# A four-stage transformer block on one Trainium2 core: wavelet and gate chains that overlap, keys chosen before the first FFN ends, fewer scores ahead, one mask product for two edges

## The reference

```python
x = x + wavelet(ln(x))     # q and v products, Haar transform over tokens, product of bands, back, W_out
x = x + ffn(ln(x))         # softmax over 8 experts, the top 2 kept; relu(x W1)^2 W2 of each
x = x + attention(ln(x))   # 16 heads of 8: a band of 128, the 128 top keys, the first 64 keys
x = x + ffn(ln(x))         # as the second stage
```

## Time and profile before

| | |
|---|---|
| Median of 3 runs | 576.11 us (575.75 to 577.48) |
| The profiled execution | 576.57 us, span 574.7 us |
| PE busy | 519.8 us, 90% |
| VectorE busy | 407.0 us, 71% |
| ACT busy | 350.0 us, 61% |
| GpSimd busy | 271.6 us, 47% |
| DMA | 32.01 MB, mean 56 GB/s |

### The profile page before, as it was taken

One profiled execution on the slowest core, in us unless ns is written; L12 is line 12 of the kernel. 1 busy time (PEld: TensorE's weight loads), 2 busy tenths in 40 slices (PEclk: granted clock), 3 DMA queues, 4 the chain that ended last, 5 costly groups with the idle time before them and its releaser, 6 DMA issues.

```text
span 574.7 us, 13509 instructions
## 1 busy us (share of the span) xinstructions
PE 519.8 (90%) x4611; PEld 326.3 (57%) x4611; DVE 407.0 (71%) x1458; ACT 350.0 (61%) x775; POOL 271.6 (47%) x429
## 2 busy tenths in 40 slices
PE   5899999999895799889998999999998999889996
PEld 2477777766663464445444554455545554477875
DVE  2545666668999789999977869878688785144335
ACT  6477665756541147656865576776765657666763
POOL 1401101430702996754426987659926346264540
PEclk9999999999897779999999999999999999999999
DMA  7970000000000000000000000001100011575606
GB/s 231 348 249 2 1 1 1 0 2 2 11 2 0 14 14 11 7 15 13 14 4 14 13 14 4 15 14 33 34 3 15 12 45 43 190 255 168 211 19 184
DMA packets 33444, 32.01 MB, mean 56 GB/s; under 512 B 7250, under 2 KB 28502, under 8 KB 33376
## 3 DMA queue, kind: packets, MB, share of 16 engines
q1 hardware_dynamic: 31616, 27.80, 15.7%
q0 software_dynamic: 1760, 3.35, 1.6%
HBM read 8.57 MB, written 12.00 MB: 36 GB/s over the span
## 4 chain that ended last, share of the span: by engine, by line
PE 57%; DVE 27%; issue 7%; POOL 3%; ACT 3%; DMA 1%; SPq 0%; DVEq 0%; POOLq 0%; ACTq 0%
PE BANK L1526 7%; PE BANK L1544 7%; DVE QST L1210 5%; PE BANK L1594 4%; PE BANK L1643 4%; PE BANK L1618 3%; PE BANK L1615 3%; DVE SW L1164 3%; PE BANK L1646 3%; PE BANK L1480 2%; PE BANK L1490 2%; DVE M L1162 2%; PE BANK L1649 2%; DVE QST L1213 2%; DVE X L1146 2%
## 5 line engine op out<-in xcount | busy, mean ns | idle before, releaser
L808 ACT ACTIVATE PT<-BANK 128x256 f32<-128x256 f32 (+2 forms) x352 | 158.6, 491 | 98.7 <-PE BANK L1618 76.0
L540 POOL TENSOR_SCALAR OH<-IOTA,POS 128x128 bf16<-128x128 bf16 x240 | 140.3, 608 | 1.6 <-DVE POS L1178 1.0
L1205 DVE CUSTOM_DVE_ANT_0 XN_a<-BANK,BANDQ 128x256 f32<-128x256 f32 (+1 forms) x128 | 62.5, 488 | 23.1 <-PE BANK L1594 20.4
L1544 PEld LDWEIGHTS BANK<-W,PT 128*128 128x128 f32 x512 | 62.5, 193 | 15.7 <-issue 14.9
L1205 DVE CUSTOM_DVE_ANT_0 XN_c<-BANK,BANDQ 128x384 f32<-128x384 f32 (+1 forms) x128 | 62.3, 487 | 8.9 <-PE BANK L1594 7.7
L1615 PE MATMUL BANK<-BANDK,IDB 128*128 128x128 bf16 x384 | 64.0, 222 | 0.6 <-ACT PT L808 0.3
L1544 PE MATMUL BANK<-W,PT 128*128 128x128 f32 x512 | 62.8, 276 | 0.0
L1526 PE MATMUL BANK<-XNT_ALL,W 128*128 128x512 f32 x128 | 62.0, 609 | 0.0
L719 ACT ACTIVATE PT<-BANK 128x512 f32<-128x512 f32 x64 | 38.0, 598 | 32.3 <-PE BANK L1526 31.7
L1615 PEld LDWEIGHTS BANK<-BANDK,IDB 128*128 128x128 bf16 x384 | 33.7, 98 | 40.2 <-ACT PT L808 22.1
L547 POOL TENSOR_TENSOR SUM<-NRM 128x128 f32<-128x128 f32 x16 | 7.3, 458 | 104.0 <-DVE NRM L1226 104.0
(11 more groups left out here) (298 smaller groups left out, 1170.7 us busy)
## 6 DMA issues: line engine op xcount, KB each, us to landing
xs<-W SPq DMA_DIRECT2D x1, 6984.0 KB, 25.5
KZB<-W SPq DMA_DIRECT2D x16, 256.0 KB, 2.4
KZC<-W SPq DMA_DIRECT2D x15, 256.0 KB, 2.3
QKV<-xs SPq DMA_DIRECT2D x31, 72.0 KB, 1.9
W<-w SPq DMA_DIRECT2D x2, 1024.0 KB, 8.6
X<-x SPq DMA_DIRECT2D x4, 256.0 KB, 3.2
out<-X SPq DMA_DIRECT2D x4, 256.0 KB, 2.2
KZB<-KALL SPq DMA_DIRECT2D x20, 36.0 KB, 1.9
```

What stands on the lines that cost most here:

```text
L540: last = nc.gpsimd.tensor_scalar(OH[g % 2][:, i, t, :], IOTA[:, :], POS[:, t, c:c + 1], None, ALU.is_equal)
L808: nc.scalar.activation(PT[u % PT_RING][:, 0:w], P2_BANK[u % SCORE_RING][:, 0:w], ACT.Exp, scale=SCALE).then_inc(S["exp_done"], 1)
L1205: nc.vector.tensor_tensor_reduce(out=JUNK[v % 2][:, 0:n], in0=P1_BANK[v % SCORE_RING][:, 0:n], in1=BANDQ[:, off:off + n], scale=1.0, scala ...
L1544: last = mm(DOWN_BANK[n % 2][:, t * P:(t + 1) * P], HID_T[n % 2][hh][:, t * P:(t + 1) * P], W2[:, e, hh, :], start=(hh == 0), stop=(hh == ...
```

## The change

Four things change. Lines of the new code lie 11 to 22 further down. In the diff, the functions `first_before` and `first_after` and the first lines behind them are VectorE's list, the loop over `with_bias` is GpSimd's, and what follows `transpose_qk(1)` is PE's.

1. **Wavelet and gate chains.** The chain of batch a + 1 starts 5 steps after that of batch a (`A_PERIOD`), not 8, so the ends and beginnings of chains lie beside the same step, and that of batch 3 ends at step (2, 3) and not at (2, 7). The gates of batches 2 and 3 are dealt out in three pieces after three steps (`GATE_SPREAD`). GpSimd's list follows.
2. **Choice of keys.** The 16 rounds begin a step earlier, 8 of them (before 4) in batch 2. Mask, marks, places and `OH` lie at (3, 5) to (3, 7). The 12 score units of group 0 that lay beside the last four steps go to the passage, behind the gathering of keys.
3. **Lead.** Four units of `p1` of group 1 are computed before the first `p2` and not eight; group 0 makes up for it (28 units beside its 22, before 24).
4. **Masks.** Where a `p2` unit has two edge blocks, one product of 256 columns writes both, and not two of 128.

```diff
+FIRST_LEAD = 4
 def scored(u):
+    if u < UNITS:
+        return UNITS_Q + FIRST_LEAD + (u + 1) * (UNITS_Q + LEAD - FIRST_LEAD) // UNITS
     return min(NG * UNITS_Q, UNITS_Q + LEAD + (u + 1) * UNITS_Q // UNITS)
...
-FIRST_ROUNDS = {(2, 4): 1, (2, 5): 1, (2, 6): 2, (3, 0): 2, (3, 1): 2, (3, 2): 2, (3, 3): 2, (3, 4): 1, (3, 5): 2, (3, 6): 1}
-FIRST_SCORES = {(3, 4): range(0, 3), (3, 5): range(3, 6), (3, 6): range(6, 9), (3, 7): range(9, 12)}
+FIRST_ROUNDS = {(2, 3): 2, (2, 4): 1, (2, 5): 1, (2, 6): 2, (2, 7): 2, (3, 0): 1, (3, 1): 1, (3, 2): 2, (3, 3): 2, (3, 4): 1, (3, 5): 1}
+MASK_AT, MARKS_AT, PLACES_AT, ONEHOT_AT = (3, 5), (3, 6), (3, 7), (3, 7)
+A_PERIOD = 5
+GATE_SPREAD = ((0, 1), (2, 3), (4, 5))
+def a_steps(b, e):
+    for a in range(1, B):
+        step = b * E + e - A_PERIOD * (a - 1)
+        if 0 <= step < E:
+            yield step, a
...
-            for b in range(B):
-                if b + 1 < B:
-                    with_bias(b + 1, 0).then_inc(S["a_xb"], 1)
-                if b:
-                    rstd("c", b - 1)
-                if b >= 2:
-                    stacks(b - 2)
-                if b + 1 < B:
-                    rstd("g", b + 1)
-                if b + 2 < B:
-                    rstd("a", b + 2)
-                if b >= 2:
-                    values(b - 2)
+            for a in range(1, B):
+                with_bias(a, 0).then_inc(S["a_xb"], 1)
+                if a + 1 < B:
+                    rstd("a", a + 1)
+                rstd("g", a)
+                if a == 2:
+                    rstd("c", 0)
+            for b in range(2, B):
+                rstd("c", b - 1)
+                stacks(b - 2)
+                values(b - 2)
...
             def first_before(b, e):
-                if b + 1 < B:
-                    a_step(e, b + 1)
-                    if e == E - 1:
-                        dve.wait_ge(S["g_comb"], b + 2)
+                for step, a in a_steps(b, e):
+                    if step < E - 1:
+                        a_step(step, a)
                 if b:
                     c_step(e, b - 1)
+                for step, a in a_steps(b, e):
+                    if step == E - 1 and a == 1:
+                        a_step(step, a)
+                if b + 1 < B and e == E - 1:
+                    dve.wait_ge(S["g_comb"], b + 2)
             def first_after(b, e):
-                if b + 2 < B and e == 5:
-                    stats("a", b + 2)
-                if b + 2 < B and e == 6:
-                    normalize("a", b + 2)
+                for k, parts in enumerate(GATE_SPREAD):
+                    for a in range(2, B):
+                        if b * E + e - A_PERIOD * (a - 1) == E - 1 + k:
+                            gate("g", a, parts)
+                for step, a in a_steps(b, e):
+                    if a + 1 < B and step == A_PERIOD - 3:
+                        stats("a", a + 1)
+                    if a + 1 < B and step == A_PERIOD - 2:
+                        normalize("a", a + 1)
                 rounds(0, 2 * FIRST_ROUNDS.get((b, e), 0))
-                maxima(FIRST_SCORES.get((b, e), ()))
-                if (b, e) == (B - 1, E - 2):
+                if (b, e) == MASK_AT:
                     mask(0)
+                if (b, e) == MARKS_AT:
+                    dve.wait_ge(S["sel_t"], 1)
+                    marks(A_BANK[0]).then_inc(S["sel_t_s"], 1)
+                if (b, e) == PLACES_AT:
+                    dve.wait_ge(S["sel_pos"], 1)
+                    places(0, A_BANK[1]).then_inc(S["sel_done"], 1)
+                if (b, e) == ONEHOT_AT:
+                    dve.wait_ge(S["sel_done"], 1)
+                    dve.wait_ge(S["consts_ready"], 1)
+                    for i in range(HG):
+                        for t in range(T):
+                            last = nc.vector.tensor_scalar(OH[0][:, i, t, :], IOTA[:, :], POS[:, t, i:i + 1], None, ALU.is_equal)
+                    last.then_inc(S["onehot_dve"], 1)
...
             c_step(0, B - 1)
+            gathered_kv(0)
+            maxima(range(0, 4))
             c_step(1, B - 1)
-            maxima(range(14, 16))
-            gathered_kv(0)
+            maxima(range(4, 16))
             maxima(range(16, 18))
...
             transpose_qk(1)
+            pe.wait_ge(S["sel_done"], 1)
+            gather_kv(0)
+            for w in range(16):
                 p1(0, w)
-            gather_kv(0)
             c_step(2, B - 1)
...
                 if r < T:
                     lo, hi = key_range(r)
-                    first = True
-                    for side, q in ((0, r - 1), (1, r + 1)):
-                        if lo <= q < hi:
-                            mm(bank[:, (q - lo) * P:(q - lo + 1) * P], IDB[:, :], BANDK[:, side, :],
-                               start=first, stop=False, skip_group_check=True)
-                            first = False
+                    if 0 < r < T - 1:
+                        edges = bank[:, 0:3 * P].rearrange("p (n q) -> p n q", n=3)[:, 0:3:2, :]
+                        mm(edges, IDB[:, :], BANDK[:, :, :], start=True, stop=False, skip_group_check=True)
+                    else:
+                        side, q = (1, 1) if r == 0 else (0, T - 2)
+                        mm(bank[:, (q - lo) * P:(q - lo + 1) * P], IDB[:, :], BANDK[:, side, :],
+                           start=True, stop=False, skip_group_check=True)
```

More of the change, by code:

```diff
@@ L988, in gate_part, with gate @@
                         link(nc.vector.reduce_sum(XROW[:, k, j, D], GK, AX_X))
-            def gate(n, b):
-                for part in range(GATE_PARTS):
+            def gate(n, b, parts=range(GATE_PARTS)):
+                for part in parts:
                     gate_part(n, b, part)
@@ L1294, in _ @@
             maxima(range(20, UNITS_Q))
-            maxima(range(UNITS_Q, UNITS_Q + LEAD))
+            maxima(range(UNITS_Q, UNITS_Q + FIRST_LEAD))
             gathered_kv(1)
@@ L1703, in first_beside @@
                     transpose_qk(0)
-                if (b, e) in FIRST_SCORES:
-                    if b == B - 1:
-                        pe.wait_ge(S["g_sub"], B)
-                    for w in FIRST_SCORES[b, e]:
-                        p1(0, w)
+                if (b, e) == MARKS_AT:
+                    pe.wait_ge(S["sel_mask"], 1)
+                    pe.wait_ge(S["g_sub"], B)
+                    sel_marks(A_BANK[0]).then_inc(S["sel_t"], 1)
+                if (b, e) == PLACES_AT:
+                    pe.wait_ge(S["sel_t_s"], 1)
+                    pe.wait_ge(S["consts_ready"], 1)
+                    sel_places(A_BANK[1]).then_inc(S["sel_pos"], 1)
             def normalized(b):
@@ L1740, in _ @@
             transpose_again(0)
-            for w in range(LEAD):
+            for w in range(FIRST_LEAD):
                 p1(1, w)
```

33 lines of the change are left out of this document (6 added, 27 removed).

## The result

The changed kernel takes 570.14 us (median of 5 runs, 570.10 to 572.99) and the kernel before, run alternately with it, 576.11 us (median of 5, 575.50 to 578.35). The ratio is 0.9905, with an interval of 0.9888 to 0.9923. The profiled execution took 570.12 us with a span of 568.3 us; before it was 574.7 us. The forecast was 572.3 us: right in direction and inside the range as a whole, but the gain is 6.0 us where 3.8 were expected. It lies outside the narrower band of 570.8 to 573.8 us that the prediction gave to the forecast itself, in the part of the range that it left to rival A.

A forecast was written before the change was run, and what follows sets the result against it. VectorE was taken to bound the stretch from 142.7 us to group 1; an earlier, shorter lane less a longer second part gave -3.8 us, 572.3 us as median. Own range 570.8 to 573.8, with rivals 568.3 to 575.5.

The forecast's parts named there:

- rival A: Passage from FFN to attention and group 0 shrink too, PE keeping 2.4 GHz longer; up to -8.6, 567.5 us; chance 0.17.
- What bounds the kernel: PE in batches 1 and 2; from 142.7 us to group 1 at 221.6, one lane of VectorE work.
- Start of the lane: VectorE's accumulation of step (2, 7) starts at 139.8 and not 142.7: -2.9 us, allowing 1.0 us of lag.
- First part of the lane: VectorE's stretch to the end of the last accumulation: 172.8 and not 180.7 us, 7.9 earlier, with 1.5 for mutual waits.
- Second part: From the last accumulation's end to group 1: 45.0 us, before 40.9; group 1 begins at 217.8, 3.8 us earlier.
- Sum: Whole kernel: 576.57 - 3.8 = 572.8 us against the profiled execution, 572.3 as median; later groups shift as a whole.
- Lead: Four maxima move from ahead of the first p2 to group 0: costs nothing, 1.7 us at most.
- Masks: Merged edge products in 16 groups, 128 fewer: columns set the pace, so 0 us, upper bound 0.4 us.
- Chains closer together: Near step (1, 0), gate, statistics and normalizings stand close; VectorE has idle time there, so 0 us.
- Rival D: Slower: PE waits in batches 0 to 2, 3.8 us each with half clock; two waits give 579.9 us; chance 0.06.
- Rival B: GpSimd's stacks hold up VectorE's gate and normalizing; 0.5 to 2.5 us reach the lane, 573 to 575; chance 0.18.

The follow-up runs named there:

- pool_waits: The change, with GpSimd starting its attention stacks only after VectorE has normalized for the next batch; 569.30 us, ratio 0.9858 to the kernel before.
- scores_late: The change, with PE's scores for the choice of keys moved behind the last four score units of group 0; 568.85 us, ratio 0.9863 to before.
- gates_whole: The change, with the gates of batches 2 and 3 in one piece again; 570.88 us, ratio 0.9885 to the kernel before.
- masks_back: The change, with two mask products of 128 columns again for one of 256; 592.05 us on a slower chip (before 599.03), ratio 0.9889.
- busy_gap: The change, with 30 useless products in PE's wait for the one-hot rows; 570.02 us, ratio 0.9872 to the kernel before.

## Why the prediction was right, and where its size was off

*What bounds the kernel: right.* That VectorE sets the stretch to group 1 shows in what was taken off it: 1.9 us less of normalizing behind (2, 7) gave 1.10 us at the last accumulation (`pool_waits`), up to PE's own limit, and 1.02 us less of waiting gave 0.8 at group 1 (`scores_late`).

*Start of the lane: right.* 140.43 forecast as 139.8. Of the allowed lag of 1.0 us, 1.6 came, on PE: the product for `VG` started at 138.93 and not at 137.33, and VectorE waited 1.18 us for PE at 135.61. Of the 1.6 us, 0.93 were there at the first FFN's first product, ahead of anything that the change moves on PE; 0.45 are a wait for `XN_g` at 78.5; 0.2 aren't traced. VectorE itself kept up in batch 2 although GpSimd held up the gate's products.

*First part of the lane: right in sum, with luck.* The last accumulation ends at 172.9 and was forecast at 172.8, but three terms were off and cancel. PE came 1.6 us late to the product for `VG`. PE's own limit, from that product to the end of the last accumulation, was put at 34.0 us (137.33 to 171.3); `pool_waits`, where PE never idles, shows 32.9. And of the 1.5 us allowed for waits of the two engines on each other, 1.1 came, the difference between the change and `pool_waits`. That is 1.6 - 1.1 - 0.4 = 0.1 us.

*Second part: the term that was mis-sized.* It was put at 45.0 us (40.9 + 3.9 - 0.3 + 0.5) and was 42.7, which is under the 43 us that the prediction had set as a sign of being wrong on the passage. By VectorE's rows, its work grew by 3.04 us and not by 3.6: the one-hot rows took 2.69 and not 2.91 us, and 16 maxima without a wait between them take 0.42 us each and not 0.43. Its idle time was put at 5.87 + 0.5 and came to 4.63. About 1.0 us of that is the clock: with the same list and the late return it is 43.6 us in `gates_whole` (44.74 less the 1.1 of accumulation). This is a part of rival A, to which the prediction gave 0.17: PE came back to full clock at 185 us, ahead of q/k/v, and at 194 before, when the first four of them (2.93 us) were done. It is not that PE "keeps" the level from a denser FFN, as rival A put it: it lost it at 175 us, 5 us earlier than before, in its wait of 3.80 us, and had it back earlier too. The gathering cost 0.25 us and not 0.5. Of the 2.3 us that are 0.5 for VectorE's work, 1.0 for the clock and 0.25 for the gathering; what is left, some 0.5 us, is spread over waits that were summed as staying what they were, and isn't resolved further.

*Sum.* -6.08 us at group 1, where -3.8 was forecast; -0.12 in the later groups; -0.2 behind them; 6.4 us in the span of the two profiles and 6.0 in the medians. From the FFN's first product it is -7.0 at group 1. That compares a profiled execution of the change in which the clock came back early with one of the kernel before that had the lower of its two mean clocks (0.978). Kernels with the change's list and a late clock (`masks_back`, `busy_gap`, `gates_whole`) have -5.9 to -6.2.

*Lead: right* (0). *Masks: right within the bound of 0.4 us, but not nothing.* The groups are 0.12 us shorter together, which just passes the 0.1 us that was to be the sign of being wrong. The first four take 0.04 us less, the same in all traces; at that rate sixteen would be 0.16 us, an estimate. A mask product of 256 columns starts 0.12 us before the next product, as two of 128 did:

```profile
256.63 0.28 PE L1635 MATMUL BANK<-BANDK,IDB 128*128 128x256 bf16 x1
256.75 0.33 PE L1640 MATMUL BANK<-QT,PR 128*128 128x384 f16 x1
```

By the figure of the Trainium skill (TensorE: Matmul & The Clock Gate, "Wait — 56ns, not 53.3ns?") 0.3 us was to be had. The traces show 0.12 us over the groups, and 0.16 by the estimate: about half of that.

*Chains closer together: right.* One new wait, 0.45 us at 78.5 for `XN_g`, and a clock of 1.00 throughout. Rival D didn't come.

*Rival B: its mechanism is there, its cost isn't.* The gate's products were held up by 2 us, as the Trainium skill (SBUF — State Buffer, "Who interferes with whom") says for two inputs from SBUF beside a GpSimd instruction that reads it; the trace agrees, with 0.96, 0.75 and 0.82 us in place of 0.19, 0.43 and 0.42. Batch 2 had the slack for it. Where the slack was gone (`XN_c` of batch 2, 3.03 us, and 3.20 before), `pool_waits` shows the price: 1.1 us at the last accumulation.

*What the prediction didn't see* is that its parts hang together. It added a term for the chains and a term for the moved maxima. At the last accumulation, from the FFN's first product, they give 1.95 and 4.07 us alone and 8.7 together. Each removes one set of PE's waits, and the other set is enough to keep the stretch long and to bring the clock down once. The times of the runs are too coarse to show this.

## What to carry to other kernels

Where two engines hand a bound to and fro, list the waits of the engine that is waited for in the whole stretch, and ask which remain if only one cause is taken away: here the parts gave 6.0 us at the end of the stretch when tried one by one, and 8.7 together. Count positions from an event ahead of which nothing was changed, not from the start of the span: that start moved by over 1 us here. Where an engine sits near full in a stretch, look at the waits of the other one for the order of its list first (a move of four products that take 1 us gave 0.8 us here), and at its clock second. And give a forecast for a stretch at low clock a spread of its own: the moment at which the clock returns moved by 3 us with nothing changed in PE's list there.
